# The attention's value projection: f32 products replaced by three fp32r products of split operands

## The chip, the core and the metric

The kernel runs on one core of one Trainium2 chip. The metric is the device time of one launch in microseconds (us); the median of three runs of the kernel before is 1106.51 us (1106.11 to 1109.37).

## The reference, cut to what matters

The program is a chain of two layers on x of shape (4, 256, 256), 1024 rows of 256 features. Each layer has a graph-like stage and a feed-forward stage. The change touches the attention of the last stage:

```python
h = _rmsnorm(hidden_states, ln1_w)          # hidden_states: (4, 256, 256)
q = (h @ Wq).reshape(B, S, NH, HD)          # NH = 32 heads, HD = 128
k = (h @ Wk).reshape(B, S, KVH, HD)         # KVH = 4 heads of keys and values
v = (h @ Wv).reshape(B, S, KVH, HD)         # <- the values: 1024x256 @ 256x512
q, k = _rope(q, pos), _rope(k, pos)
k, v = jnp.repeat(k, rep, axis=2), jnp.repeat(v, rep, axis=2)   # rep = 8
scores = jnp.einsum('bqhd,bkhd->bhqk', q, k) / jnp.sqrt(jnp.float32(HD))
...                                          # causal mask, softmax
o = jnp.einsum('bhqk,bkhd->bqhd', attn, v).reshape(B, S, NH * HD) @ Wo
```

After it comes a mixture of 32 experts and a shared one, which takes the last 280 us or so.

## The kernel before, in words

The kernel is written engine by engine: each engine has its own instruction stream, and the streams meet at named semaphores (`S["..."]`). Graph attention comes first, then a sparse mixture, then a learned mixing, then the attention touched here, then the mixture of 33 experts.

The attention runs over 8 blocks. A block is one of 4 groups g (one key/value head and its 8 query heads) and one half of the rows (512 rows, two of the four batches); block blk = 2g + half. Each block has 16 units u (8 heads by 2 batches), and each engine walks a software pipeline over steps k from -7 to 134, unit u starting at about step u. In step k the TensorE stream does, in this order: `turn(k-2)` (three transposes of the probabilities, L964), `scores(k+1)` (two products, L954), a projection job where one is due, `weigh(k-3)` (probabilities by values, L975 and L976) and `project_out(k-5)` (six products with the output weights, L57 to L59).

The projection jobs of a block are ten, and `JOB_AT` says at which steps they stand: job 0 at step 16 blk - 7 projects the values, job 1 the keys, jobs 2 to 9 the queries of the 8 heads. `project(n, blk, i)` writes one PSUM bank of 128x512.

Jobs 1 to 9 use **split operands**. An f32 number is written as high + low; ScalarE makes the high part by copying into the type fp32r, and GpSimd (weights) or VectorE (activations) makes the low part by a subtraction. `split_product` (L57, L58, L59) then issues three fp32r products: high by high, high by low, low by high. The activations are split once for all blocks into `actT_r`; the query and key weights of a group into `wqk_r` (`high_weights` L1245 on ScalarE, `low_weights` L1450 on GpSimd), the output weights into `wo_r` (L1265, L1464). Each job has 6 such products of 512 moving columns; `project_out` has 6 of 256.

Job 0 is different: it multiplies plain f32, 4 row tiles by 2 halves of the contraction, 8 products of 128 moving columns (L933), with the activations as stationary operand and the value weights `wv_g` as moving operand. The program shows each f32 product as two LDWEIGHTS and MATMUL pairs, so a job 0 has 16 pairs; an fp32r product is one pair. `wv_g` holds the weights of one group, loaded by `load_values(g)` (L506) from SyncE's queue, which waits until job 0 of block 2g-1 is done. VectorE's `cosines` copies the finished bank to `vt` (L1996) and frees the bank (`q_taken`).

ScalarE and GpSimd reach each split by the step at which it is due: `wqk_part_in(k)` and `wo_part_in(k)` give group and part.

Of the kernel before, what the change touches and what calls it, by code (L numbers as in the profile page):

```python
# [14 lines left out]
P = 128  # L15
# [3 lines left out]
HC = D // P  # L19
# [5 lines left out]
NH, KV, HD = 32, 4, 128  # L25
# [19 lines left out]
F32 = mybir.dt.float32  # L45
F32R = mybir.dt.float32r
# [54 lines left out]
def build(nc, x, ctxT, W0, W1, a_self0, a_neigh0, a_self1, a_neigh1, b01,  # L101
          w_router, w_gate, w_up, w_down, WqT, WkT, gamma, ln1, ln2, Wq, Wk, Wv, Wo, Wr, ebias,
          Wg, Wu, Wd, ident_in, ind_in, rope_q, rope_k, causal_in, before_in, out):
    with ExitStack() as ctx:
# [165 lines left out]
        def sb_resting(name, shape):  # L270
# [22 lines left out]
        wo_g = sb("wo_g", [P, REP, D])  # L293
        gate_w = sb("gate_w", [P, 2, HC, I1])
        up_w = sb("up_w", [P, 2, HC, I1])
        down_w = sb("down_w", [P, 2, I1 // P, D])

        x_rows = nc.dram_tensor("x_rows", (T * P, D), F32, kind="Internal").ap()
# [26 lines left out]

            "logit_ready", "rexp_done", "rmax_done", "sq_done", "ms_done", "rms_done", "norm2_done", "norm2T_ready", "x3_added",
            "gu1", "silu1", "hid1", "down1", "acc1", "whi1", "wlo1", "hidf1", "hidh1", "actT_hi", "actT_lo",
            "wqk_hi", "wqk_lo", "wo_hi", "wo_lo",

            "q_ready", "q_swapped", "q_taken", "q_sin", "q_rot",  # L330
            "s_ready", "s_shift", "p_exp", "p_inv", "p_norm", "pT_ready", "pT_copied",
# [99 lines left out]
        def wqk_part_in(k):  # L431

            g, p = divmod(k + 2 * BU - 4, 2 * BU)
            return (g, p // 2) if 1 <= g < KV and p % 2 == 0 and p // 2 < len(WQK_PARTS) else None

        def wo_part_in(k):

# [9 lines left out]
        def _(sp):  # L447
# [89 lines left out]
            for g in range(1, KV):  # L537
                sp.wait_ge(S["wqk_lo"], len(WQK_PARTS) * g)
                load_queries(g)
                sp.wait_ge(S["wo_lo"], REP // 2 * g)  # L540
                load_output(g)
                sp.wait_ge(S["q_ready"], ((2 * g - 1) * JOBS) + 1)
                load_values(g)

            load_experts(1)
# [9 lines left out]
        def _(pe):  # L555
# [361 lines left out]
            def attention():  # L917

                def project(n, blk, i):
                    g, half = divmod(blk, 2)  # L920
                    dst = Q_BANK[n % 2]
                    if n >= 2:
                        pe.wait_ge(S["q_taken"], n - 1)
                    if i == 0:
                        pe.wait_ge(S["wv_in"], 16 * g + 16)
                        for j in range(4):
                            t = 4 * half + j
                            if n == 0 and j == 2:
                                turn_rows_norm(2)
                                turn_rows_norm(3)  # L930
                            pe.wait_ge(S["normT_copied"], T + t // 2 * 2 + 2)
                            for c in range(HC):
                                mm = pe.matmul(dst[:, j * HD:j * HD + HD], actT[:, c, t * P:t * P + P], wv_g[:, c, :],  # L933
                                               start=c == 0, stop=c == HC - 1)
                        mm.then_inc(S["q_ready"], 1)
                        return
                    pe.wait_ge(S["actT_lo"], half + 2)
                    pe.wait_ge(S["wqk_lo"], len(WQK_PARTS) * g + 1 + i // 2)
                    cols = slice((i - 1) * HD, i * HD)
                    for c in range(HC):  # L940
                        mm = split_product(
                            pe, dst[:], [wqk_r[:, g % 2, j, c, cols] for j in range(2)],
                            [actT_r[:, j, c, half * 512:half * 512 + 512] for j in range(2)], c == 0, c == HC - 1)
                    mm.then_inc(S["q_ready"], 1)

                def scores(u):
                    blk, g, half, r, b2 = unit_of(u)
                    b = 2 * half + b2
                    if b2 == 0:
                        pe.wait_ge(S["q_rot"], turned(blk, 2 + r) + 1)  # L950
                    if u >= 2:
                        pe.wait_ge(S["s_shift"], u - 1)
                    for nt in range(NT):
                        mm = pe.matmul(S_BANK[u % 2][:, nt * P:nt * P + (nt + 1) * P],  # L954
                                       qT[:, (u // 2) % 4, b2 * N + nt * P:b2 * N + nt * P + P],
                                       kT[:, b * N:b * N + (nt + 1) * P], start=True, stop=True)
                    mm.then_inc(S["s_ready"], 1)

                def turn(u):
                    pe.wait_ge(S["p_norm"], u + 1)  # L960
                    if u >= 1:
                        pe.wait_ge(S["pT_copied"], u)
                    for j in range(3):
                        mm = pe.transpose(PT_BANK[:, j * P:j * P + P], prob[:, u % 4, j * P:j * P + P], ident[:])  # L964
                    mm.then_inc(S["pT_ready"], 1)

                def weigh(u):
                    blk, g, half, r, b2 = unit_of(u)
                    t = NT * (2 * half + b2)
                    pe.wait_ge(S["pT_copied"], u + 1)  # L970
                    if u % BU == 0:
                        pe.wait_ge(S["q_taken"], blk * JOBS + 1)
                    if u >= 1:
                        pe.wait_ge(S["o_copied"], u)
                    pe.matmul(O_BANK[:, 0:N], vt[:, t, :], probT[:, u % 2, 0:N], start=True, stop=False)  # L975
                    pe.matmul(O_BANK[:, P:N], vt[:, t + 1, :], probT[:, u % 2, N:N + P],  # L976
                              start=False, stop=True).then_inc(S["o_ready"], 1)

                def project_out(u):
                    blk, g, half, r, b2 = unit_of(u)  # L980
                    pe.wait_ge(S["o_copied"], u + 1)
                    if half == 0:
                        pe.wait_ge(S["wo_lo"], REP // 2 * g + 1 + r // 2)
                    if r == 0 and blk >= 1:
                        pe.wait_ge(S["wo_added"], 2 * (blk - 1) + b2 + 1)
                    if u < 2:
                        pe.wait_ge(S["normT_copied"], 2 * T)
                    for nt in range(NT):
                        mm = split_product(
                            pe, W_BANK[b2][:, nt * D:nt * D + D],  # L990
                            [o_ring[:, u % O_RING, j, nt * P:nt * P + P] for j in range(2)],
                            [wo_r[:, g % 2, j, r, :] for j in range(2)], r == 0 and nt == 0, r == REP - 1 and nt == NT - 1)
                    mm.then_inc(S["o_used"], 1)

                for k in range(FIRST, END):
                    if 0 <= k - 2 < AU:
                        turn(k - 2)
                    if 0 <= k + 1 < AU:
                        scores(k + 1)
                    if (q := job_in(k)) is not None:  # L1000
                        project(*q)
                    if k in (AU - 7, AU - 6):
                        turn2(2 * (k - AU + 7))
                        turn2(2 * (k - AU + 7) + 1)
                    if k == AU - 4:
                        logits(0)
                    if k in (AU - 1, AU + 1, AU + 3):
                        s = (k - AU + 1) // 2
                        gate_up(s, s)
                    if 0 <= k - 3 < AU:  # L1010
                        weigh(k - 3)
                    if 0 <= k - 5 < AU:
                        project_out(k - 5)
                    for t in {-1: (4, 5), 1: (6, 7)}.get(k, ()):
                        turn_rows_norm(t)
# [21 lines left out]
        def _(act):  # L1037
# [200 lines left out]
            def high_weights(g, p):  # L1238
# [5 lines left out]
                src = wk_g[:] if p == 0 else wq_g[:, :, 2 * HD * (p - 1):2 * HD * p]  # L1244
                act.activation(wqk_r[:, g % 2, 0, :, WQK_PARTS[p]], src, ACT.Copy).then_inc(S["wqk_hi"], 1)  # L1245

            def attention():
                act.wait_ge(S["att_in"], 48)

# [39 lines left out]
                for k in range(FIRST, END):  # L1289
# [7 lines left out]
                        exps(k)  # L1297
                    if (part := wqk_part_in(k)) is not None:
                        high_weights(*part)
                    if (part := wo_part_in(k)) is not None:  # L1300
                        high_outputs(*part)
                    if k == -7:
# [71 lines left out]
        def _(pool):  # L1374
# [70 lines left out]
            def low_weights(g, p):  # L1445
# [4 lines left out]
                pool.tensor_tensor(wqk_r[:, g % 2, 1, :, WQK_PARTS[p]], src,  # L1450
                                   wqk_r[:, g % 2, 0, :, WQK_PARTS[p]].bitcast(F32), ALU.subtract).then_inc(S["wqk_lo"], 1)

            def inverse_rms(p):

                sl = slice(2 * p, 2 * p + 2)
                pool.wait_ge(S["sq_done"], 2 * p + 2)
                pool.tensor_scalar(ms[:, sl], ms[:, sl], EPS, None, ALU.add).then_inc(S["ms_done"], 1)
                pool.wait_ge(S["ms_done"], p + 1)
                pool.tensor_tensor(rms[:, sl], ms[:, sl], minus_half[:], ALU.pow).then_inc(S["rms_done"], 1)
# [50 lines left out]
            for k in range(FIRST, END):  # L1510
                if (q := job_in(k, 1)) is not None:
                    sines(*q)
                if (part := wqk_part_in(k)) is not None:
                    low_weights(*part)
                if (part := wo_part_in(k)) is not None:
                    low_outputs(*part)
                if k in (AU - 10, AU - 9, AU + 5, AU + 6):
# [656 lines left out]
```

## Time and profile before

| | |
|---|---|
| median of 3 runs | 1106.51 us |
| the profiled execution's own time | 1106.92 us |
| its span | 1105.1 us |
| mean granted TensorE clock | 0.945 of full speed |
| PE busy | 1008.7 us (91%) |
| PEld (weight loads) busy | 823.0 us (74%) |
| DVE busy | 868.7 us (79%) |
| ACT busy | 614.3 us (56%) |
| POOL busy | 423.4 us (38%) |

PE is TensorE's matmul side and PEld its weight-load side, which runs beside it; DVE is VectorE, ACT ScalarE, POOL GpSimd, SP SyncE. The recorded time of one MATMUL holds its way through the array, so it is longer than the distance from one MATMUL to the next; where the prediction needs the cost of a product, it takes this distance. TensorE's granted clock has two levels, 1.2 and 2.4 GHz, shown as 0.50 and 1.00.

### The profile page before, as it was taken

The page shows a single profiled execution, that of the slowest core. Times are in us where ns is not written, and L with a number is a line of the kernel's source. Part 1 is how long each engine was busy: PE and PEld are TensorE (multiplying, and loading weights), DVE is VectorE, ACT ScalarE, POOL GpSimd, SP SyncE. Part 2 cuts the span into 40 slices and gives each one's busy share as a digit, 9 for nine tenths or more (in the row PEclk, how much of TensorE's full clock was granted, in tenths as well). Part 3 has the DMA queues.
Part 4 walks back from the last instruction along what each step waited for, and adds up shares of the span by engine and source line. Part 5 has one row for each costly group of instructions (what it writes and reads, how often), then busy time and mean ns, then how long its engine had stood idle before and what let it go on. Part 6 is the DMA issues. An engine that isn't in the chain of part 4 may idle for free.

```text
span 1105.1 us, 20158 instructions
## 1 busy us (share of the span) xinstructions
PE 1008.7 (91%) x5934; PEld 823.0 (74%) x5934; DVE 868.7 (79%) x2639; ACT 614.3 (56%) x1746; POOL 423.4 (38%) x365
## 2 busy tenths in 40 slices
PE   4797877999995489999999999999999999999997
PEld 2454545466663368999999999999887888888886
DVE  6999996577763889877777867777878888888877
ACT  4789983533332377777786777777952222222221
POOL 5788892611113433333332333312422233233221
PEclk9869887699998689999999999999999999999999
DMA  9700003111111311010101000000010111111111
GB/s 294 247 1 2 1 2 110 29 44 48 48 34 58 120 39 49 1 40 1 48 1 40 12 24 1 1 1 2 15 30 23 49 43 47 52 43 43 57 43 38
DMA packets 50258, 49.23 MB, mean 45 GB/s; under 512 B 5024, under 2 KB 43488, under 8 KB 50176
## 3 DMA queue, kind: packets, MB, share of 16 engines
q1 hardware_dynamic: 47024, 41.74, 11.8%
q0 software_dynamic: 1872, 5.11, 1.7%
q10 hardware_dynamic: 1280, 1.38, 0.5%
q8 instruction: 40, 0.66, 0.2%
q14 instruction: 42, 0.34, 0.1%
HBM read 43.10 MB, written 5.11 MB: 44 GB/s over the span
## 4 chain that ended last, share of the span: by engine, by line
PE 72%; DVE 10%; POOL 8%; ACT 4%; issue 4%; DMA 1%; SPq 0%; DVEq 0%; ACTq 0%; POOLq 0%
PE bank L57 13%; PE bank L58 13%; PE bank L59 13%; PE bank L954 6%; PE bank L975 5%; PE bank L849 4%; PE bank L857 4%; PE bank L876 4%; PE bank L964 3%; POOL rest L1411 3%; PE bank L976 2%; POOL alpha L1414 2%; POOL ytok L1506 1%; DVE alpha L1614 1%; PE bank L643 1%
## 5 line engine op out<-in xcount | busy, mean ns | idle before, releaser
L1476 POOL TENSOR_TENSOR rot_s<-swap,rq 128x512 f32<-128x512 f32 x64 | 88.5, 1383 | 194.8 <-ACT swap L1258 194.7
L1134 ACT ACTIVATE silu<-bank 128x512 f32<-128x512 f32 x66 | 39.5, 599 | 175.2 <-PE bank L59 175.2
L2049 DVE TENSOR_TENSOR o_ring<-bank,o_ring 128x256 fp32r<-128x256 f32 x128 | 54.3, 424 | 80.1 <-ACT o_ring L1287 78.7
L1271 ACT ACTIVATE prob<-prob,pmin 128x128 f32<-128x128 f32 (+1 forms) x256 | 113.3, 447 | 5.5 <-DVE pmin L2030 5.5
L954 PE MATMUL bank<-kv,norm 128*128 128x128 f32 (+1 forms) x512 | 106.0, 330 | 6.9 <-DVE norm L2023 6.8
L1872 DVE SCALAR_TENSOR_TENSOR xs<-bank,wt,xs 128x256 f32<-128x256 f32 x264 | 109.0, 476 | 0.1
L1432 POOL TENSOR_TENSOR gate_r<-gate_w,gate_r 128x256 fp32r<-128x256 f32 x31 | 36.4, 1175 | 177.3 <-ACT gate_r L1127 177.3
L1287 ACT ACTIVATE o_ring<-bank 128x256 fp32r<-128x256 f32 x128 | 48.4, 378 | 76.3 <-PE bank L976 76.2
L57 PE MATMUL bank<-wo_r,o_ring 128*128 128x256 f32 x256 | 82.4, 322 | 0.0
L1850 DVE TENSOR_TENSOR hidf<-silu,bank 128x512 f32<-128x512 f32 x66 | 45.4, 688 | 46.4 <-ACT silu L1134 44.8
L2042 DVE TENSOR_SCALAR prob<-prob,pinv 128x128 f32<-128x128 f32 (+1 forms) x256 | 77.1, 343 | 4.6
L2030 DVE CUSTOM_DVE_ANT_0 prob<-bank,causal 128x128 f32<-128x128 f32 (+1 forms) x256 | 80.3, 352 | 0.1
L975 PE MATMUL bank<-probT,kv 128*128 128x256 f32 x256 | 76.9, 382 | 3.3 <-DVE o_ring L2049 3.3
L1066 ACT ACTIVATE alpha<-alpha,edge_min 128x256 f32<-128x256 f32 x128 | 64.8, 527 | 19.1 <-DVE edge_min L1614 11.9
L57 PE MATMUL bank<-actT_r,wqk_r 128*128 128x512 f32 x144 | 71.8, 499 | 2.8 <-DVE kv L1996 2.8
L954 PEld LDWEIGHTS bank<-kv,norm 128*128 128x128 f32 x512 | 68.0, 193 | 7.6 <-DVE norm L2023 7.5
L57 PE MATMUL bank<-down_r,hidT 128*128 128x256 f32 x248 | 70.2, 283 | 2.7 <-DVE xs L1872 1.4
L59 PE MATMUL bank<-wo_r,o_ring 128*128 128x256 f32 x256 | 72.2, 282 | 0.0
L58 PE MATMUL bank<-wo_r,o_ring 128*128 128x256 f32 x256 | 72.1, 281 | 0.0
L1614 DVE CUSTOM_DVE_ANT_0 alpha<-alpha,norm 128x256 f32<-128x256 f32 x128 | 69.8, 581 | 2.6 <-POOL alpha L1414 2.2
L1281 ACT ACTIVATE probT<-bank 128x384 f32<-128x384 f32 x128 | 62.8, 491 | 13.5 <-PE bank L964 7.9
L59 PE MATMUL bank<-down_r,hidT 128*128 128x256 f32 x248 | 70.2, 283 | 0.0
(300 smaller groups left out, 3080.6 us busy)
## 6 DMA issues: line engine op xcount, KB each, us to landing
gate_w<-in_Wg SPq DMA_DIRECT2D x33, 128.0 KB, 2.1
up_w<-in_Wu SPq DMA_DIRECT2D x33, 128.0 KB, 2.2
down_w<-in_Wd SPq DMA_DIRECT2D x33, 128.0 KB, 2.3
w_all<-in_w_gate SPq DMA_DIRECT2D x8, 512.0 KB, 10.5
w_all<-in_w_up SPq DMA_DIRECT2D x8, 512.0 KB, 10.4
w_all<-in_w_down SPq DMA_DIRECT2D x8, 512.0 KB, 10.6
wq_g<-in_Wq SPq DMA_DIRECT2D x4, 1024.0 KB, 5.5
wo_g<-in_Wo SPq DMA_DIRECT2D x4, 1024.0 KB, 5.3
```

What stands on the lines that cost most here:

```text
L57: pe.matmul(out, lhs[0], rhs[0], start=first, stop=False)
L58: pe.matmul(out, lhs[0], rhs[1], start=False, stop=False)
L59: return pe.matmul(out, lhs[1], rhs[0], start=False, stop=last)
L954: mm = pe.matmul(S_BANK[u % 2][:, nt * P:nt * P + (nt + 1) * P], qT[:, (u // 2) % 4, b2 * N + nt * P:b2 * N + nt * P + P], kT[:, b * N:b * ...
L975: pe.matmul(O_BANK[:, 0:N], vt[:, t, :], probT[:, u % 2, 0:N], start=True, stop=False)
L1066: ins = act.activation(alpha[:, k % RING, nt * N:nt * N + N], alpha[:, k % RING, nt * N:nt * N + N], ACT.Exp, bias=edge_min[:, k % RING, n ...
L1271: ins = act.activation(prob[:, u % 4, nt * P:nt * P + (nt + 1) * P], prob[:, u % 4, nt * P:nt * P + (nt + 1) * P], ACT.Exp, bias=pmin[:, u ...
L1476: pool.tensor_tensor(rot_s[:, m % 2].rearrange("p (b n) -> p b n", b=2), swap[:, m % 2].rearrange("p (b n) -> p b n", b=2), bcast(tab[:, 1 ...
L1614: ins = dve.tensor_tensor_reduce(out=alpha[:, k % RING, nt * N:nt * N + N], in0=alpha[:, k % RING, nt * N:nt * N + N], in1=adj[:, r % B, n ...
L1872: ins = dve.scalar_tensor_tensor(xs[:, t, :], DB[2 * (mod % 2) + j // 2][:, j % 2 * D:j % 2 * D + D], w, xs[:, t, :], ALU.mult, ALU.add)
L2030: ins = dve.tensor_tensor_reduce(out=prob[:, u % 4, nt * P:nt * P + (nt + 1) * P], in0=S_BANK[u % 2][:, nt * P:nt * P + (nt + 1) * P], in1 ...
L2042: ins = dve.tensor_scalar(prob[:, u % 4, nt * P:nt * P + (nt + 1) * P], prob[:, u % 4, nt * P:nt * P + (nt + 1) * P], pinv[:, u % 4, nt:nt ...
```

## The change

A new tile `wv_r` holds the high and low parts of one group's value weights. ScalarE makes the high part (`high_values`) and GpSimd the low part (`low_values`), once a group: for group 0 at the first two steps of the pipeline, for the others at step 32g - 14 (`wv_in`). From block 1 on, job 0 multiplies `actT_r` by `wv_r` with `split_product`: 4 row tiles by 2 halves by 3, which is 24 fp32r products of 128 moving columns in place of 8 f32 products. Block 0 keeps the f32 products. `load_values(g)` waits in addition for the split of group g-1.

```diff
+        wv_r = sb("wv_r", [P, 2, HC, HD], F32R)
...
+        def wv_in(k):
+
+            g, p = divmod(k + 14, 2 * BU)
+            return g if 1 <= g < KV and p == 0 else None
...
                 sp.wait_ge(S["q_ready"], ((2 * g - 1) * JOBS) + 1)
+                sp.wait_ge(S["wv_lo"], g)
                 load_values(g)
...
+                    if i == 0 and blk > 0:
+                        pe.wait_ge(S["wv_lo"], g + 1)
+                        pe.wait_ge(S["actT_lo"], half + 2)
+                        for j in range(4):
+                            t = 4 * half + j
+                            for c in range(HC):
+                                mm = split_product(pe, dst[:, j * HD:j * HD + HD],
+                                                   [actT_r[:, q, c, t * P:t * P + P] for q in range(2)],
+                                                   [wv_r[:, q, c, :] for q in range(2)], c == 0, c == HC - 1)
+                        mm.then_inc(S["q_ready"], 1)
+                        return
...
+            def high_values(g):
+
+                act.wait_ge(S["wv_in"], 16 * g + 16)
+                act.activation(wv_r[:, 0], wv_g[:], ACT.Copy).then_inc(S["wv_hi"], 1)
...
+                    if k == FIRST:
+                        high_values(0)
+                    if (g := wv_in(k)) is not None:
+                        high_values(g)
...
+            def low_values(g):
+
+                pool.wait_ge(S["wv_hi"], g + 1)
+                pool.tensor_tensor(wv_r[:, 1], wv_g[:], wv_r[:, 0].bitcast(F32), ALU.subtract).then_inc(S["wv_lo"], 1)
...
+                if k == FIRST + 1:
+                    low_values(0)
+                if (g := wv_in(k)) is not None:
+                    low_values(g)
```

## Rows read from the trace of the kernel before

**Rows 1.** The page: the span in 40 equal slices, busy tenths and granted clock.

```profile
PE   4797877999995489999999999999999999999997
DVE  6999996577763889877777867777878888888877
PEclk9869887699998689999999999999999999999999
```

**Rows 2.** Windows from attention on: length, busy of each engine (instructions), clock, DMA, GB/s.

```profile
365.00:420.00 55.00, 40.07 (x190) 32.66 (x191) 47.00 (x139) 33.48 (x94) 22.50 (x18) 0.81 0.21 70
475.20:527.10 51.90, 51.90 (x343) 47.90 (x342) 39.35 (x150) 39.57 (x119) 17.06 (x14) 1.00 0.07 21
527.10:579.00 51.90, 51.90 (x343) 47.90 (x342) 39.35 (x150) 40.31 (x120) 18.89 (x15) 1.00 0.09 27
421.00:440.00 19.00, 18.43 (x122) 16.48 (x121) 18.61 (x62) 13.26 (x38) 6.46 (x5) 1.00 0.15 44
```

**Rows 3.** Waits of PE from 421 to 475: total us, times, longest.

```profile
PE bank L975 <- DVE o_ring L2049: 0.8, 3, 0.3
```

**Rows 4.** Timeline of PE around job 0 of block 2: start, length, instruction.

```profile
474.54 0.82 PE L954 MATMUL bank<-kv,norm 128*128 128x128 f32 x4
475.19 1.95 PE L933 MATMUL bank<-wv_g,actT 128*128 128x128 f32 x16
476.98 0.60 PE L975 MATMUL bank<-probT,kv 128*128 128x256 f32 x2
```

**Rows 5.** Timeline of PE: fp32r products of 256, then of 512 columns.

```profile
441.41 0.28 PE L58 MATMUL bank<-wo_r,o_ring 128*128 128x256 f32 x1
...
441.88 0.28 PE L59 MATMUL bank<-wo_r,o_ring 128*128 128x256 f32 x1
...
443.57 0.39 PE L58 MATMUL bank<-actT_r,wqk_r 128*128 128x512 f32 x1
...
444.50 0.40 PE L59 MATMUL bank<-actT_r,wqk_r 128*128 128x512 f32 x1
```

**Rows 6.** Timeline of PE around the router's products of 32 columns.

```profile
794.75 0.82 PE L954 MATMUL bank<-kv,norm 128*128 128x128 f32 x4
795.41 1.87 PE L798 MATMUL bank<-wr,actT 128*128 128x32 f32 x16
```

**Rows 7.** One line each, weight loads: least, median, greatest ns, first and last start.

```profile
L798 PEld LDWEIGHTS bank<-wr,actT x32: 188/192/192, 795.2 to 835.8; 128*128 128x128 f32 x32
L57 PEld LDWEIGHTS bank<-wo_r,o_ring x256: 187/192/193, 410.7 to 820.6; 128*128 128x128 f32 x128
```

**Rows 8.** One tile, the split of the key weights, in the same columns.

```profile
L1245 ACT ACTIVATE wqk_r<-wk_g x4: 401/402/417, 192.7 to 615.8; 128x256 fp32r<-128x256 f32 x4
L1450 POOL TENSOR_TENSOR wqk_r<-wk_g,wqk_r x4: 728/736/781, 205.4 to 616.3; 128x256 fp32r<-128x256 f32 x4
```

**Rows 9.** Timelines of ACT and of POOL at the pipeline's start.

```profile
372.90 0.30 ACT L1228 ACTIVATE sd<-mv,eps 128x2 f32<-128x2 f32 x1 [3.34 <-DVE mv L1934]
...
376.99 1.49 POOL L1464 TENSOR_TENSOR wo_r<-wo_g,wo_r 128x512 fp32r<-128x512 f32 x1 [8.53 <-ACT wo_r L1265]
```

**Rows 10.** Timelines of ACT and of POOL about step 18.

```profile
455.42 0.39 ACT L1287 ACTIVATE o_ring<-bank 128x256 fp32r<-128x256 f32 x1 [0.74 <-PE bank L976]
...
457.10 1.57 POOL L1476 TENSOR_TENSOR rot_s<-swap,rq 128x512 f32<-128x512 f32 x1 [2.43 <-ACT swap L1258]
460.78 1.29 POOL L1464 TENSOR_TENSOR wo_r<-wo_g,wo_r 128x512 fp32r<-128x512 f32 x1 [2.11 <-ACT wo_r L1265]
```

**Rows 11.** Timeline of SP's queue: the value weights of group 1.

```profile
423.35 0.37 SPq L506 DMA_DIRECT2D wv_g<-in_Wv  x1
```

More of the change, by code:

```diff
@@ L327, in build @@
             "gu1", "silu1", "hid1", "down1", "acc1", "whi1", "wlo1", "hidf1", "hidh1", "actT_hi", "actT_lo",
-            "wqk_hi", "wqk_lo", "wo_hi", "wo_lo",
+            "wqk_hi", "wqk_lo", "wo_hi", "wo_lo", "wv_hi", "wv_lo",
             "q_ready", "q_swapped", "q_taken", "q_sin", "q_rot",
```

## The prediction

> **What bounds the kernel now.** I read four views, from wide to narrow. First the 40 slices: from the tenth slice on, PE stands at 8 or 9 tenths almost everywhere, with a dip where the attention begins [rows 1]. Second the windows, cut at job 0 of each block. From 475.2 on a block of the attention takes 51.90 us and PE is busy for all 51.90 of them, while DVE has 39.35, ACT 39.57 and POOL 17.06; the clock is 1.00 [rows 2]. The reader is to see that a busy PE says nothing by itself, since recorded matmuls overlap, so I asked, third, who makes PE wait: between 421 and 475 it is VectorE three times, 0.8 us in all [rows 3], and from 475 to 735 the view of waits has no line for PE at all. Fourth, the timeline of PE around one value job: the products before, in and after it follow each other with no idle time named [rows 4]. So from block 2 on TensorE's stream is the path that sets the end, and a ns added to it there is a ns of the kernel. Before 421 that isn't so: in 365 to 420 PE is busy for 40.07 of 55 us and DVE for 47.00, at a mean clock of 0.81 [rows 2]. The change leaves the value job of that stretch (block 0) as it is.
>
> **What the job costs now.** The recorded time of these products holds the way through the array, so I measure from the end of the last product before to the end of the job's last. The scores end at 474.54 + 0.82 = 475.36, the job at 475.19 + 1.95 = 477.14: 1.78 us for 16 pairs, 0.111 us a pair, 0.223 us for one f32 product of 128 columns [rows 4]. This goes in seven of the eight blocks.
>
> **What it costs after.** 24 pairs, each a load of 128x128 weights and an fp32r product of 128 columns. The trace has fp32r products of 256 and 512 columns: from 441.41 to 441.88 there are four steps, 0.118 us each, and from 443.57 to 444.50 four, 0.233 us each [rows 5]. The difference, 0.115 us for 256 columns, gives 0.45 ns a column, and drawn on to 128 columns 0.060 us. That would be the end below: 24 x 0.060 = 1.44 us, 0.34 us less than now.
>
> But each pair also loads weights, and the trace shows what a pair costs when the stream is short. The router's logits are 16 f32 pairs of 32 columns with 128x128 weights. Scores before them end at 794.75 + 0.82 = 795.57, they at 795.41 + 1.87 = 797.28: 1.71 us, 0.107 us a pair [rows 6]. Thirty-two columns are a quarter of the 128 of the value job, yet the pair is hardly shorter than its 0.111. What is left as its bound is the weight load. The load of fp32r weights is recorded as long as that of f32 weights, 187 to 193 ns against 188 to 192 [rows 7], so I take it that the fp32r pair has the same floor. It is also why fp32r pays with 256 columns: there the stream of 0.118 us covers a load of 0.107.
>
> The Trainium skill ("TensorE: Matmul & The Clock Gate", "LDWEIGHTS (loading the stationary operand)") gives the same floor from its side, the columns of the stationary operand divided by 1.2, in ns, which is an estimate of 107 ns here; the 0.107 us of the router's pairs agrees. The same page ("Back-to-back issue gap") speaks against a floor this high: it says that a sustained stream of loads and products of 128 columns goes at about 81 ns a pair. By it the job would take an estimated 24 x 0.081 = 1.94 us and the kernel would become longer by an estimated 1.1 us over seven blocks; the f32 pairs here, 0.111, don't show it.
>
> So an fp32r pair of 128 columns lies between 0.107 (the router's pair) and 0.118 (the 256-column pair, which can't be shorter than one of 128). I take 0.112, the value job's own with its 1.784 / 16 rounded up: 24 x 0.112 = 2.69 us against 1.78, or 0.91 us more for each job. The ends are 24 x 0.107 = 2.57 (0.79 more) and 24 x 0.118 = 2.83 (1.05 more).
>
> There is an end above that no row excludes. No row has an fp32r product between 8 and 256 columns. Should a short fp32r product stream no faster than a whole f32 product, it costs 0.223 us, and the job 24 x 0.223 = 5.35 us, 3.57 more.
>
> **Where it falls.** Blocks 2 to 7: six jobs on a PE that never waits, 6 x 0.91 = 5.5 us. Block 1's job stands at 421.37, in a stretch where DVE is busy for 18.61 of 19.00 us [rows 2] and PE waits for it three times afterwards, 0.8 us [rows 3]. A longer job lets DVE catch up, so between nothing and all of the 0.91 is paid; I take 0.3, near the lower end since waits of 0.8 stand against it.
>
> **The splits.** By the split of a key weight, the same shape, one costs 0.40 us on ACT and 0.74 us on POOL [rows 8]; it is made four times. For group 0, ACT stands idle for 3.34 us before its roots at 372.90, and the new copy comes just ahead of them in its queue; POOL stands idle for 8.53 us until 376.99, waiting for the first output weights [rows 9]. Behind POOL's new instruction are those output weights and then the sines of the keys, and both come after the idle time. So group 0's split is free; with the cover gone it would cost 0.40 + 0.74 = 1.1 us once. For groups 1 to 3 it is due at step 32g - 14, the first of them near 453 us (seven steps of 51.9/16 = 3.24 us ahead of the job at 475.19). There ACT has idle times of 0.74 us and POOL of 2.43 and 2.11 [rows 10]; behind the copy on ACT wait the next high part of the attention's output and the swaps, and PE has room for them because block 3, in which POOL is busy 1.83 us longer and ACT 0.74 longer than in block 2, is as long as block 2 to the hundredth [rows 2]. Price zero, at most 3 x 0.4 = 1.2 us if each copy were to delay PE in full.
>
> **The waits.** PE's new wait for the low part has 18 us of slack at block 2 and likewise later. Its wait for the activations' low part asks for what job 1 of the same half asks for already; in blocks 1 and on that was made before step 9. SP's new wait stands behind one for job 0 of block 2g - 1, and the split it asks for is by then some 50 us old or more (371 to 423 for group 0); the load is issued at 423.35 [rows 11] and its reader comes at 453. Behind it in SP's queue is the next group's load of queries, due much later. All free, and nothing below nothing, for these only add waits.
>
> **The sum.** 5.5 + 0.3 + 0 + 0 = 5.8 us more. Against the profiled execution that is 1106.9 + 5.8 = 1112.7 us; its span is 1105.1, so 1.8 us lie around it, which I leave. The median shown is 0.4 lower than the profiled execution, so I predict 1106.5 + 5.8 = 1112.3 us. The likeliest case's own range: 6 x 0.79 + 0 = 4.7 to 6 x 1.05 + 1.05 + 1.2 = 8.6 more, so 1111 to 1115.
>
> **The rivals.**
> *Short fp32r products stream slowly.* Seven jobs by 3.57 us are 25.0 us more, 1131.5 us; block 1 then has no wait left to swallow it. For it: the rows know fp32r to be cheap only at 256 columns and more. Against it: at those lengths it goes at one rate, with no sign of a fixed cost that a short one would feel. Chance 0.23.
> *The weight load isn't a floor for fp32r* (this one ends on the other side). It would decide wherever a pair costs less than 1.78/24 = 0.074 us; at 0.060 the kernel gains 0.34 us in each of the last six blocks and up to that in block 1, 2.0 to 2.4 in all: 1104.3 us. For it: three products of 1 x 128 columns stream less than two passes of the f32 kind (0.180 against 0.223 us). Against it: the equal times of the loads [rows 7] and the router's 0.107 [rows 6]. Chance 0.08.
> *A partly hidden load.* At a pair between 0.074 and 0.095 us the job costs 1.8 to 2.3 us, the kernel 0 to 3.3 us more, some 1108. This is where the figure of 81 ns from the Trainium skill's page on TensorE's back-to-back issue gap would put it, as told above. The rows speak against it as they do against the case before. Chance 0.09.
> *The job isn't on the path after all*, because VectorE takes over as the bound: DVE has 12.55 us free in a block, so a longer PE only eases it. Chance 0.02, at 1107 us.
>
> **How the numbers follow.** The likeliest case has 0.58. The range is to take in the slow stream above (0.23), so it ends at 1132, and it leaves out the gain and most of the partly hidden load below, so it begins at 1108; it holds about 0.85. This kernel's measurement can tell about 0.3%, or 3.3 us, from no change. Slower by over 3.3 us: 0.58 + 0.23 = 0.81. Within 3.3 us: the partly hidden load, the gain of 2 us and the longer job that costs nothing, 0.19, of which I give 0.03 away to faster by over 3.3 us, which no case gives, for what I don't see.
>
> **What would show it.** In the changed kernel's timeline job 0 of block 2 has 24 MATMULs of 128 columns, from end to end 2.6 to 2.8 us (slow stream: 5.4; load hidden: 1.4). The windows of blocks 2 to 7 grow from 51.90 to about 52.8 us each with PE busy throughout, and PE still has no wait from 475 on. PE's three waits for VectorE after 421 shrink. ACT and POOL grow by 1.6 and 3.0 us. I am wrong if a block grows by less than 0.5 or more than 1.5 us, or if PE starts to wait for GpSimd or ScalarE near step 18, 50 or 82.

## The result, and the profile after

The changed kernel takes 1112.97 us (median of 7 runs, 1111.92 to 1116.26), the kernel before 1106.51 in the same set (7 runs, 1105.92 to 1109.37). The ratio is 1.0059, 95% interval 1.0049 to 1.0069, so 6.5 us slower, where 5.8 us were forecast. A ratio, here and below, is the recorded estimate from the runs of both kernels and need not be the quotient of the two medians; where a difference is given "by the ratio", it is that estimate applied to the median of before. Its profiled execution spans 1111.2 us, 6.1 more than that of before.

The page's slices of the changed kernel look as before's [rows 1], and from block 1 of the attention on the granted clock stands at 9, which is 90% of full speed or more, in every slice:

```profile
PE   4777867999995589999999999999998999999997
PEclk9988886699998699999999999999999999999999
```

The windows of blocks 2 and 3 come next, cut at job 0 as in [rows 2], and under them the stretch in which VectorE had been the bound; the columns are those of [rows 2].

```profile
475.81:528.61 52.80, 52.80 (x352) 48.78 (x351) 39.34 (x149) 39.58 (x119) 17.06 (x14) 1.00 0.06 21
528.61:581.42 52.81, 52.81 (x352) 48.80 (x351) 39.36 (x149) 40.63 (x121) 19.64 (x16) 1.00 0.08 26
421.00:440.00 19.00, 18.90 (x128) 17.05 (x127) 18.61 (x58) 12.79 (x39) 6.55 (x5) 1.00 0.11 27
```

A block is 0.90 us longer than the 51.90 of before, and PE is busy for all of it, as before. DVE and ACT do what they did. In block 3 POOL has 0.75 us and ACT 0.32 us more than before, which is that block's split, and the block is no longer than block 2 for it.

The job itself, in the timeline of PE at block 2, answers to [rows 4]:

```profile
475.34 0.82 PE L972 MATMUL bank<-kv,norm 128*128 128x128 f32 x4
475.81 0.41 PE L57 MATMUL bank<-wv_r,actT_r 128*128 128x128 f32 x1
476.05 0.28 PE L58 MATMUL bank<-wv_r,actT_r 128*128 128x128 f32 x1
476.17 0.27 PE L59 MATMUL bank<-wv_r,actT_r 128*128 128x128 f32 x1
...
478.51 0.28 PE L59 MATMUL bank<-wv_r,actT_r 128*128 128x128 f32 x1
478.62 0.65 PE L993 MATMUL bank<-probT,kv 128*128 128x256 f32 x2
```

Measured as the prediction measures, from the recorded end of the scores (475.34 + 0.82 = 476.16) to that of the job (478.51 + 0.28 = 478.79), this is 2.63 us, within the 2.6 to 2.8 forecast. There are 24 products, and from the second (476.05) to the last (478.51) they stand 2.46 / 22 = 0.112 us apart. The record of each still says 0.27 or 0.28 us; as in all these rows, it is the distance of starts that prices a product, not its recorded length.

The waits of PE from 421 to 475, against [rows 3], and the tile `wv_r` by itself (least, median, greatest ns, first and last start), against [rows 7] and [rows 8]:

```profile
PE bank L993 <- DVE o_ring L2085: 0.3, 1, 0.3
```

```profile
L57 PEld LDWEIGHTS bank<-wv_r,actT_r x56: 190/192/192, 421.6 to 742.3; 128*128 128x128 f32 x56
L57 PE MATMUL bank<-wv_r,actT_r x56: 272/277/411, 421.6 to 742.3; 128*128 128x128 f32 x56
...
L1268 ACT ACTIVATE wv_r<-wv_g x4: 402/404/431, 369.9 to 666.6; 128x256 fp32r<-128x256 f32 x4
L1483 POOL TENSOR_TENSOR wv_r<-wv_g,wv_r x4: 725/732/734, 370.5 to 667.1; 128x256 fp32r<-128x256 f32 x4
```

Where the 6.1 us of span came from is measured between the starts of the scores (L954 before, L972 in the changed kernel) ahead of each job 0. The job's own start won't do where jobs of two kinds are compared: the f32 job's first record stands 0.65 us behind the start of those scores (474.54 to 475.19), the fp32r job's 0.47 us (475.34 to 475.81).

| stretch, between starts of scores | before | after | more |
|---|---|---|---|
| start of the span to block 1's | 420.71 | 421.14 | 0.43 |
| block 1's to block 2's | 53.83 | 54.20 | 0.37 |
| block 2's to block 7's, five blocks | 259.56 | 264.03 | 4.47 |
| block 7's to the router's | 60.65 | 61.56 | 0.91 |
| the router's to the end | 310.35 | 310.27 | -0.08 |

So each of the last six blocks pays 0.89 to 0.91 us, 5.38 together, and block 1 pays 0.37. The 0.43 us ahead of block 1 come before the first changed job; only group 0's split stands there.

### The profile page after: what moved, and what is told of

It reads as the page before. It is cut to its first block, busy times and chain, and to the rows that moved or that the text cites. A ratio compares the mean times of both kernels' runs of the same rounds, so it can differ in the third digit from the quotient of the medians.

```text
span 1111.2 us, 20281 instructions
## 1 busy us (share of the span) xinstructions
PE 1010.7 (91%) x5990; PEld 826.7 (74%) x5990; DVE 869.5 (78%) x2639; ACT 615.2 (55%) x1750; POOL 426.7 (38%) x369
## 4 chain that ended last, share of the span: by engine, by line
PE 72%; POOL 11%; DVE 8%; issue 4%; ACT 4%; DMA 1%; SPq 0%; DVEq 0%; POOLq 0%; ACTq 0%
PE bank L57 13%; PE bank L58 13%; PE bank L59 13%; PE bank L972 7%; PE bank L993 5%; POOL rest L1438 5%; PE bank L856 4%; PE bank L864 4%; PE bank L883 4%; PE bank L982 3%; POOL alpha L1441 3%; PE bank L994 2%; POOL ytok L1538 1%; DVE alpha L1650 1%; PE bank L875 1%
## 5 line engine op out<-in xcount | busy, mean ns | idle before, releaser
L972 PE MATMUL bank<-kv,norm 128*128 128x128 f32 (+1 forms) x512 | 106.1, 331 | 5.5 <-DVE norm L2059 5.5
L972 PEld LDWEIGHTS bank<-kv,norm 128*128 128x128 f32 x512 | 68.0, 193 | 6.6 <-DVE norm L2059 6.5
```

## The experiments

Ratios are against the kernel before in the same set of runs: its median was 1107.64 us beside the first four kernels recorded (e1 to e4) and 1108.5 beside the others. Each kernel is the changed one but for the edit shown, and the last is the kernel before with an edit. Since the stretch ahead of block 1 differs by up to 5.2 us between profiled executions, the second measure of each is the distance from block 2's to block 3's job 0, which repeats to 0.06 us or better from block to block. Two kernels with job 0 of the same kind are compared by it directly.

**Only the splits.** Everything beside TensorE stays as in the change, and TensorE goes back to f32.

```diff
-                    if i == 0 and blk > 0:
+                    if i == 0 and blk < 0:
```

> The value weights are split as in the change (ScalarE's copy, GpSimd's subtraction, SyncE's wait), but TensorE's job 0 stays f32 in every block. Theory (all of the loss is TensorE's longer value job): blocks of 51.9 us and a time equal to that of before, within 1 us (1106.5). Rival (the copies or the waits delay the pipeline): up to 1.2 us from the copies, and if most of the 6.5 us came from them, 1109 to 1113.

Measured: 1107.89 us against 1107.64, ratio 1.0003 (0.9992 to 1.0014). Blocks of 51.92 us (476.16 to 528.08). The splits and the waits cost nothing that can be measured, at most 1.6 us by the interval, and in the trace 320.22 us go from block 2's job to the router's products (476.16 to 796.38), as before (475.19 to 795.41). The growth of the blocks is TensorE's longer job.

**64 moving columns.**

```diff
-                                mm = split_product(pe, dst[:, j * HD:j * HD + HD],
+                                mm = split_product(pe, dst[:, j * HD:j * HD + HD // 2],
                                                    [actT_r[:, q, c, t * P:t * P + P] for q in range(2)],
-                                                   [wv_r[:, q, c, :] for q in range(2)], c == 0, c == HC - 1)
+                                                   [wv_r[:, q, c, 0:HD // 2] for q in range(2)], c == 0, c == HC - 1)
```

> Job 0 from block 1 on has its 24 fp32r products, but each streams only 64 of the 128 columns of the value weights (the other half of the values is left out). Theory (the load of the stationary operand, 128 columns, sets the distance of a pair): a pair stays at 0.107 to 0.111 us, a job at 2.6 to 2.7 us, the kernel at about 1113. Rival (a short fp32r product streams at two cycles a column, and the load is hidden): a pair takes 0.056 us, a job 1.3, and seven jobs end 0.44 us shorter each than the f32 ones: about 1103.5.

Measured: 1114.84 us against 1107.64, ratio 1.0057 (1.0043 to 1.0072), blocks of 52.78 us (479.60 to 532.38). Half of the values is left out. The timeline of PE in this kernel, two products of the job in block 2:

```profile
479.82 0.28 PE L58 MATMUL bank<-wv_r,actT_r 128*128 128x64 f32 x1
...
480.94 0.28 PE L59 MATMUL bank<-wv_r,actT_r 128*128 128x64 f32 x1
```

Ten steps in 1.12 us, 0.112 each: half the stream, the same price. So the stream of a short fp32r product is not what costs.

**64 stationary columns.**

```diff
-                                mm = split_product(pe, dst[:, j * HD:j * HD + HD],
-                                                   [actT_r[:, q, c, t * P:t * P + P] for q in range(2)],
+                                mm = split_product(pe, dst[0:P // 2, j * HD:j * HD + HD],
+                                                   [actT_r[:, q, c, t * P:t * P + P // 2] for q in range(2)],
```

> Job 0 has its 24 fp32r products of 128 moving columns, but loads only 64 of the 128 columns of the stationary operand (half of each row tile is left out). Theory (the load sets the distance): the load halves to about 0.054 us and the stream of 0.060 us takes over, a job of 1.4 to 1.5 us, the kernel 2 to 2.5 us faster than before, about 1104. Rival (the stream of a short fp32r product is what takes 0.111): nothing changes against the changed kernel, 1113.

Measured: 1107.5 us against 1107.64, ratio 0.9994 (0.9984 to 1.0005), blocks of 51.59 us (480.39 to 531.98). Half of each row tile is left out. The timeline of PE in block 2 and the loads of the tile:

```profile
480.64 0.23 PE L58 MATMUL bank<-wv_r,actT_r 128*64 128x128 f32 x1
...
480.94 0.22 PE L57 MATMUL bank<-wv_r,actT_r 128*64 128x128 f32 x1
```

```profile
L57 PEld LDWEIGHTS bank<-wv_r,actT_r x56: 134/136/137, 426.6 to 739.8; 128*64 128x64 f32 x56
```

Five steps in 0.30 us, 0.060 each, with the same 24 products and the same 128 moving columns; the load is recorded 56 ns shorter, 136 against 192. For 64 columns fewer that is 0.875 ns a column, and drawn on to 128 columns an estimate of 0.112 us a load, which is the distance of the pairs. At 64 columns the load would take 0.056, and the 0.060 measured is the stream's own rate, which the prediction had drawn out of the 256 and 512 column products as 0.060. The two experiments together show the floor: the distance follows the stationary columns and not the moving ones. The time fell by less than expected: 0.7 us by the ratio, 0.1 by the medians, at most 1.8 by the interval, where 2 to 2.5 were expected. The blocks give 6 x 0.31 = 1.9, and block 1 gives nothing (426.59 to 480.39, 53.80 us against 53.82), which the expectation had not allowed for. The rest of what is missing isn't in the blocks from 1 on; in the profiled execution block 1's job starts at 426.59 against 421.37, with the same work before it but for a split. The last section says what the traces show of that stretch; what the other executions did in it isn't recorded.

**Two products.** Low by high is left out, 16 pairs remain.

```diff
-                                mm = split_product(pe, dst[:, j * HD:j * HD + HD],
-                                                   [actT_r[:, q, c, t * P:t * P + P] for q in range(2)],
-                                                   [wv_r[:, q, c, :] for q in range(2)], c == 0, c == HC - 1)
+                                pe.matmul(dst[:, j * HD:j * HD + HD], actT_r[:, 0, c, t * P:t * P + P],
+                                          wv_r[:, 0, c, :], start=c == 0, stop=False)
+                                mm = pe.matmul(dst[:, j * HD:j * HD + HD], actT_r[:, 0, c, t * P:t * P + P],
+                                               wv_r[:, 1, c, :], start=False, stop=c == HC - 1)
```

> Of the three products the low part of the activations by the high part of the weights is left out: 16 pairs in job 0 in place of 24, as many as the f32 job has. Theory (only the number of pairs counts, at 0.111 us each): a job of 1.78 us and a time equal to that of before within 1 us, 1106.5. Rival (fp32r pairs cost more or less than f32 passes, or something beside TensorE costs): 16 pairs at the full stream rate of 0.060 would give 0.96 us a job and 1101; anything beside TensorE would leave it at 1108 or more.

Measured: 1110.35 us against 1107.64, ratio 1.0018 (1.0007 to 1.0029). The blocks do what the theory says: 51.88 us from 476.62 to 528.50, and four more to 736.15 at 51.91. The time doesn't: it is 2.0 us above before by the ratio. That misses the theory's 1 us and is what the expectation called 1108 or more, something beside TensorE's pairs. So the same kernel ran again.

> The kernel with two of the three products once more, since its blocks were as long as those of before (51.91 us) and its time still 0.18% above. If that excess is something of this kernel outside the attention it comes back, ratio 1.001 to 1.003; if it was drift between launches the ratio is 1.000 within 0.001.

Measured: 1109.7 us against 1108.5, ratio 1.0013 (1.0001 to 1.0024). The excess came back, smaller and just clear of nothing. The profiled execution of this run and that of the run before each span 1105.0 us, as before's 1105.1 does, and took 1106.9 us, near the lowest of its runs, so the traces can't show the excess of the others: PE has no wait between 480 and 735 in either. Nor are the two equal to before in all parts: block 1's job starts at 422.8 and 422.7, 1.4 and 1.3 us later than in before, and the stretch behind the router is 1.6 shorter than before's (last section). What the slower executions do stays open, and that the fp32r pairs cause it isn't shown: the kernel with the splits alone (1.0003, 0.9992 to 1.0014) has an interval that overlaps with both. If the changed kernel has this excess too, it is in its 6.5 us.

**One product.** Only high by high is left, 8 pairs.

```diff
-                                mm = split_product(pe, dst[:, j * HD:j * HD + HD],
-                                                   [actT_r[:, q, c, t * P:t * P + P] for q in range(2)],
-                                                   [wv_r[:, q, c, :] for q in range(2)], c == 0, c == HC - 1)
+                                mm = pe.matmul(dst[:, j * HD:j * HD + HD], actT_r[:, 0, c, t * P:t * P + P],
+                                               wv_r[:, 0, c, :], start=c == 0, stop=c == HC - 1)
```

> Only the product of the high parts is left in job 0 from block 1 on: 8 pairs of 128 columns. Theory (0.111 us a pair on a TensorE that never waits): a job of 0.89 us, 0.89 less than the f32 one; six to seven jobs: 5.3 to 6.2 us faster than before (ratio 0.9945 to 0.9952). Rival (VectorE becomes the bound once TensorE is shorter): less than half of that.

Measured: 1104.06 us against 1108.5, ratio 0.9954 (0.9936 to 0.9972), 5.1 us less by the ratio and 4.4 by the medians, under the expected 5.3 to 6.2 but well over half of it, so the rival falls. Block 1 gave nothing (53.80 us from 425.72 to 479.52, against 53.82) with PE waiting for VectorE for 1.8 us between 425 and 480, and six blocks by 0.89 are 5.3. The windows of blocks 2 and 3:

```profile
479.52:530.54 51.02, 51.02 (x337) 47.00 (x335) 39.28 (x149) 39.61 (x119) 17.08 (x14) 1.00 0.07 22
530.54:581.56 51.02, 51.02 (x337) 47.01 (x335) 39.27 (x149) 40.67 (x121) 19.65 (x16) 1.00 0.09 27
```

Blocks of 51.02, 51.91 and 52.81 us with 8, 16 and 24 pairs: 0.89 and 0.90 us for each 8, 0.112 us a pair, on a straight line. The f32 kernel, whose 16 pairs of this trace are its 8 products in two passes, lies on the same point as 16 fp32r pairs.

**Wide moving operand.**

```diff
-                        for j in range(4):
+                        for j in range(2):
                             t = 4 * half + j
                             for c in range(HC):
-                                mm = split_product(pe, dst[:, j * HD:j * HD + HD],
+                                mm = split_product(pe, dst[:, j * 2 * HD:j * 2 * HD + 2 * HD],
                                                    [actT_r[:, q, c, t * P:t * P + P] for q in range(2)],
-                                                   [wv_r[:, q, c, :] for q in range(2)], c == 0, c == HC - 1)
+                                                   [wv_r[:, q].rearrange("p c n -> p (c n)") for q in range(2)], c == 0, c == HC - 1)
```

> The changed kernel with job 0 from block 1 on as 12 fp32r products of 256 moving columns in place of 24 of 128: two row tiles of the four are multiplied by both halves of the split value weights laid side by side, so the values are wrong and as many columns stream as before; it prices the form alone. Theory (a load of 0.107 us hides under 256 columns): 12 x 0.118 = 1.42 us a job, 0.36 less than the f32 job and 1.27 less than the changed one; seven jobs: about 2.5 us faster than before. Rival (the load is paid beside the stream whatever its length): 12 x 0.22 = 2.7 us, as slow as the changed kernel.

Measured: 1106.03 us against 1108.5, ratio 0.9976 (0.9963 to 0.9989), 2.7 us less by the ratio, where about 2.5 were expected. Two of the four row tiles are left out, so this prices the form and is no whole kernel. The timeline of PE in block 2, the second and the last of the twelve products, and the window of that block:

```profile
479.94 0.28 PE L58 MATMUL bank<-wv_r,actT_r 128*128 128x256 f32 x1
...
481.14 0.28 PE L59 MATMUL bank<-wv_r,actT_r 128*128 128x256 f32 x1
```

```profile
479.63:531.20 51.57, 51.57 (x341) 47.55 (x339) 39.37 (x149) 39.61 (x119) 17.11 (x14) 1.00 0.07 22
```

Ten steps in 1.20 us, 0.120 each, for twice the columns of the change's 0.112. The loads are hidden, and the three-product form now costs less than f32: 0.33 us by this window, 0.40 by the four after it (51.51 on average up to 737.22). Block 1 gave nothing here either (53.82 us from 425.81 to 479.63).

**Groups 2 and 3 together: a whole kernel in the wide form.** Its core, with `JOB_LIST` in place of the fixed ten jobs a block; group 3's values stand in the tile `route`, idle in the attention, and the two groups' f32 weights in `gate_w`, idle until the experts.

```diff
+        JOB_LIST = sorted([(blk * BU + at, blk, i) for blk in range(BLOCKS) for i, at in enumerate(JOB_AT) if i or blk < 6]
+                          + [(3 * BU + 6, 4, -1), (4 * BU + 6, 5, -1)])
...
+                    if i <= 0 and blk > 3:
+                        pe.wait_ge(S["wv_lo"], 1)
+                        pe.wait_ge(S["actT_lo"], half + 2)
+                        for j in range(2):
+                            t = 4 * half + (0 if i < 0 else 2) + j
+                            for c in range(HC):
+                                mm = split_product(pe, dst[:, j * 2 * HD:(j + 1) * 2 * HD],
+                                                   [actT_r[:, q, c, t * P:t * P + P] for q in range(2)],
+                                                   [wv_r[:, q, c, :] for q in range(2)], c == 0, c == HC - 1)
```

> A whole kernel. Blocks 0 to 3 keep the f32 value jobs of before. The values of groups 2 and 3 are projected together: four jobs of 12 fp32r products of 256 moving columns (two row tiles by the columns of both groups), two before block 4 (steps 54 and 57) and two before block 5 (70 and 73), none in blocks 6 and 7. Theory: four jobs of 1.42 in place of 1.78 us, 1.4 us less, 1106.2 against 1107.6 (ratio 0.9987). Rival: VectorE's two copies in place of one (0.1 to 0.2 us more each) or the job at the new step make TensorE wait and eat it: no difference or slower.

Measured: 1106.4 us against 1108.5, ratio 0.9984 (0.9969 to 0.9998), 1.8 us faster than before by the ratio and, the change standing at 1.0059, faster than it. The gain over before is small and its interval ends close to 1; the profiled execution spans 1105.0 us, before's 1105.1. In the trace a job goes from 582.99 (end of the scores before) to 584.41, 1.42 us as priced. From block 2's job to the router's products it takes 319.37 us against 320.22 of before, 0.85 less where 1.44 was expected; nearly all of the rest goes to one wait that before doesn't have, in block 6, which has no value job:

```profile
686.64 0.82 PE L987 MATMUL bank<-kv,norm 128*128 128x128 f32 x4
687.84 0.67 PE L1008 MATMUL bank<-probT,kv 128*128 128x256 f32 x2 [0.38 <-DVE o_ring L2096]
```

The first product by the values starts 1.20 us behind the scores' start. The same two products of this kernel at 735.00 and 735.66, with no job and no wait between them, are 0.66 apart, so the wait, recorded as 0.38, put the stream 0.54 us back, of the 0.59 that are missing. That is the expectation's rival in part: once TensorE's work in a block shrinks, VectorE holds it up.

## Why the prediction was right

- *TensorE is the bound from block 2 on.* Right: the blocks grow by 0.90 us with PE busy throughout, no wait of PE stands between 475 and 735, and eight pairs fewer make a block 0.89 us shorter. The rival by which the job isn't on the path falls with it.
- *A pair costs 0.112 us since the weight load is its floor.* Right in size, 2.68 us a job (1.78 + 0.90) against 2.69 forecast, and now shown in its cause: the 64-column load brings 0.060, the 64-column stream leaves 0.112. What the prediction took on trust, that fp32r weights load no faster than f32 ones, held. What decided was the router's row of 32 columns [rows 6]: a short stream whose price didn't fall with its length.
- *The load takes 0.107 us.* Misread, with no harm to the sum, which used the value job's 0.112. The 1.71 us divided by 16 begin at the recorded end of the scores, 0.16 us after the router's first product has started. By starts the router's pairs of 32 columns stand as far apart as all others. In the timeline of PE before, in the windows 795.72:795.73 and 797.05:797.06, the third and fourth and then the last three of its 16 products:

```profile
795.55 0.39 PE L798 MATMUL bank<-wr,actT 128*128 128x32 f32 x2
...
796.78 0.50 PE L798 MATMUL bank<-wr,actT 128*128 128x32 f32 x3
```

  From the third to the fourteenth, eleven steps in 1.23 us, 0.112 each. So the floor is 0.112 us whether 32, 64 or 128 columns stream, and the lower end of the range, 24 x 0.107, was not there.
- *The rivals.* The slow stream of short fp32r products (25 us) falls by the 0.060 of the 64 stationary columns. The hidden load falls with it: the 0.060 exists, but only when the load is halved. The partly hidden load falls by 0.112. The Trainium skill's figure of about 81 ns a pair ("TensorE: Matmul & The Clock Gate", "Back-to-back issue gap") doesn't hold for these operands, where the measured 0.112 decides. The Trainium skill's rule for the load (same page, "LDWEIGHTS (loading the stationary operand)"), columns by 1.2, gives an estimate of 107 ns, and the measured 0.112 lies 5% above it; the agreement to the ns that the prediction noted rested on the misread 0.107.
- *Six blocks by 0.91, 5.5 us.* Five by 0.89 and one by 0.91: 5.38 us.
- *Block 1 swallows most of its 0.91, I took 0.3.* It paid 0.37. The waits fell from 0.8 us to 0.3, by the 0.5 that the block didn't pay. The 0.3 was a choice between nothing and 0.91 that no row priced, so its closeness is in part luck.
- *The splits cost nothing.* Right, ratio 1.0003 for them alone. Sizes were 0.40 and 0.73 us; the one at 455.38 fills ACT's idle time, as said. On the page POOL grew by 3.3 us (3.0 forecast) and ACT by 0.9 (1.6 forecast), though the four copies themselves take 1.6.
- *The sum* of 5.8 us compares with 5.75 us of growth from block 1's scores to the router's (0.37 + 4.47 + 0.91), 6.1 us of span and 6.5 us between the medians, whose interval is 5.4 to 7.6.

What the prediction had no price for is the spread of the stretches outside the attention, which is larger than several of its terms.

## What to carry to other kernels

A product with its own stationary operand costs the longer of its stream and its weight load; with 128 stationary f32 or fp32r columns the load was 0.112 us here and longer than the stream up to 128 moving fp32r columns, so, in this kernel, three split products replace f32 ones at a gain only where the moving operand is long enough (256 columns: 3 x 0.12 = 0.36 us against 2 x 0.223 = 0.45 for the same columns as two f32 products of 128) and at a loss at 128 (3 x 0.112 against 0.223). Look in the trace for a product with a very short moving operand: the distance between starts inside such a row is the load's price, whatever the recorded lengths say. When a product can't be made longer within its job, look for another job with the same stationary operand, as the two groups' values have here.

## What was not expected of the hardware

Block 1's job starts at 421.4, 421.6, 422.4, 422.7, 422.8, 423.8, 425.4, 425.7, 425.8 and 426.6 us in the ten profiled executions, which have the same work before it but for at most one split. That spread, 5.2 us, is nearly as much as the whole change, while the blocks of one kernel agree to 0.06 us. Part of it goes with TensorE's granted clock: from block 0's job to block 1's the kernel before takes 56.00 us and the one with 64 stationary columns 58.60, with the same products in between:

```profile
365.37:421.37 56.00, 41.43 (x199) 33.75 (x199) 48.03 (x141) 34.62 (x96) 22.87 (x19) 0.81 0.20 67
367.99:426.59 58.60, 41.81 (x198) 34.23 (x199) 49.40 (x141) 34.83 (x97) 23.55 (x20) 0.79 0.19 65
```

The stretch from the router's products to the end has only two lengths. It is 309.7 and 309.6 us before and after the change, and 308.0 to 308.1 in all eight experiments. The two long ones have a piece of 3.4 us at the lower clock among the experts' products, which the others lack; before, after, and the kernel with the splits alone:

```profile
830.20:833.60 3.40, 3.40 (x10) 2.62 (x9) 1.15 (x3) 0.00 (x0) 0.00 (x0) 0.50 0.00 0
837.45:840.85 3.40, 3.40 (x12) 2.72 (x11) 0.09 (x1) 0.49 (x1) 0.00 (x0) 0.50 0.02 5
831.15:834.55 3.40, 3.40 (x21) 2.95 (x19) 1.19 (x4) 0.67 (x2) 0.00 (x0) 1.00 0.00 0
```

A wait of PE for VectorE of 1.8 us stands shortly ahead of that place in all three, so the wait alone doesn't decide it. The piece costs 1.5 to 1.7 us. Since before and after both have it, it doesn't bear on their comparison, but it does on that of a span of theirs with one of an experiment.

Also PE's busy time on the page grew by only 2.0 us (1008.7 to 1010.7) while the span grew by 6.1: in the first 200 us it fell from 148.80 to 143.63 us at a mean clock of 0.85 in place of 0.83, for nearly the same work (1012 and 1016 products). The page's total would have hidden the change; the windows between two like events showed it.
